# Two-stage mixture of experts: the second stage in 20 slots in place of 23, the last four of them split between two experts

## The reference

```python
logits = jnp.einsum('bsh,eh->bse', x, router_w)
idx = jnp.argmax(logits, axis=-1).reshape(-1)
for e in range(8):
    g = bitlinear(xf, wg[e])                  # rows to int8 steps, weights to -1, 0, 1
    u = bitlinear(xf, wu[e])
    y = bitlinear(jnp.square(jax.nn.relu(g)) * u, wd[e])
    out = out + jnp.where((idx == e)[:, None], y, 0.0)
```

## Time and profile before

| | |
|---|---|
| median of 3 runs | 249.35 us (249.04 to 249.41) |
| profiled execution | 250.49 us |
| its span | 248.4 us |
| busy PE, DVE, ACT, POOL | 90%, 87%, 83%, 67% of the span |
| moved by DMA | 55.94 MB, mean 225 GB/s |

### The profile page before, as it was taken

The page is one execution under the profiler, slowest core; times in us unless marked ns, Lnnn a source line. Parts: engine busy times, 40 slices in busy tenths (PEclk is TensorE's granted clock), DMA queues, the critical chain, the costliest instruction groups (busy, mean ns, idle before and its releaser), DMA issues.

```text
span 248.4 us, 6396 instructions
## 1 busy us (share of the span) xinstructions
PE 224.2 (90%) x1627; PEld 175.1 (70%) x1627; DVE 215.4 (87%) x702; ACT 205.5 (83%) x312; POOL 166.6 (67%) x327
## 2 busy tenths in 40 slices
PE   2398999999999999998999999987799999999970
PEld 2245788889899999998999998974344454544430
DVE  5979999967968999888988999978999999999971
ACT  2768799788767899997999978887779999999970
POOL 4262676746746698888878875555537788687863
PEclk9999999999999999999999999999889999999998
DMA  5999999987955465697566655635068982211110
GB/s 190 424 336 386 428 418 391 369 352 251 367 243 190 154 209 211 225 358 287 198 216 205 221 216 216 211 96 153 24 173 276 298 284 88 106 59 74 64 43 0
DMA packets 14304, 55.94 MB, mean 225 GB/s; under 512 B 2814, under 2 KB 2814, under 8 KB 10176
## 3 DMA queue, kind: packets, MB, share of 16 engines
q1 hardware_dynamic: 9392, 42.10, 47.3%
q0 software_dynamic: 4880, 13.44, 15.5%
HBM read 44.68 MB, written 13.48 MB: 234 GB/s over the span
## 4 chain that ended last, share of the span: by engine, by line
PE 76%; DVE 13%; issue 5%; POOL 2%; ACT 2%; DMA 1%; DVEq 0%; POOLq 0%; ACTq 0%
PE banks L1726 39%; PE banks L1903 20%; PE banks L1709 8%; PE banks L1895 2%; PE banks L2007 2%; PE banks L1871 2%; PE banks L1751 2%; POOL out_rows L719 1%; PE banks L1779 1%; DVE row L1247 1%; DVE ternary L1049 1%; DVE p L1227 1%; DVE stats L1191 1%; DVE hT_lo L1220 1%; DMA token_ids<-token_ids_in 1%
## 5 line engine op out<-in xcount | busy, mean ns | idle before, releaser
L1903 PE MATMUL banks<-ternary,qT 128*128 x184 | 47.6, 389 | 1.5 <-ACT qT L863 1.4
L774 ACT ACTIVATE ternary<-staged 128x2048 bf16<-128x2048 f32 x20 | 38.1, 1905 | 3.1 <-DMA staged<-weight_chunks 3.1
L780 ACT ACTIVATE ternary<-staged,w_scale 128x1536 int16<-128x1536 f32 (+1 forms) x20 | 34.4, 1725 | 2.9 <-DVE w_scale L1144 2.9
L1903 PEld LDWEIGHTS banks<-ternary,qT 128*128 128x128 bf16 x184 | 17.5, 100 | 17.6 <-issue 2.7
L633 POOL DMA_INDIRECT x_rows<-row,store_at x19 | 22.6, 1191 | 9.3 <-POOL store_at L625 6.6
L1726 PE MATMUL banks<-ctx_hi,pT_hi 128*128 x132 | 22.8, 312 | 2.5 <-DVE row L1247 1.1
L1903 PE MATMUL banks<-ternary,rT 128*128 x92 | 23.7, 380 | 1.3 <-ACT rT L887 0.8
L535 POOL DMA_INDIRECT x<-x_rows,gather x16 | 18.3, 1141 | 9.3 <-DVE gather L1061 6.4
L719 POOL DMA_INDIRECT out_rows<-late_rows,late_token x18 | 19.2, 1069 | 7.7 <-DVE late_rows L1498 5.5
L588 POOL TENSOR_TENSOR row<-ln,half_powers 128x2 f32<-128x2 f32 x19 | 14.1, 744 | 13.6 <-DVE squares L1262 13.6
L1726 PE MATMUL banks<-ctx_hi,hT_hi 128*128 x132 | 22.8, 311 | 0.0
(11 more groups left out here) (253 smaller groups left out, 627.2 us busy)
## 6 DMA issues: line engine op xcount, KB each, us to landing
staged<-weight_chunks SPq DMA_DIRECT2D x20, 1024.0 KB, 6.4
late_rows<-x_rows SPq DMA_DIRECT2D x18, 260.0 KB, 3.6
ternary<-ctx_chunks SPq DMA_DIRECT2D x4, 1024.0 KB, 8.2
ternary<-weight_chunks SPq DMA_DIRECT2D x4, 1024.0 KB, 10.0
ternary<-ctx_rows SPq DMA_DIRECT2D x4, 1024.0 KB, 13.0
x_rows<-filler SPq DMA_DIRECT2D x1, 2080.0 KB, 13.9
staged<-x_rows SPq DMA_DIRECT2D x5, 260.0 KB, 3.1
x_rows<-row,store_at POOLq DMA_INDIRECT x19, 3.8
```

Of the source, the lines that this page charges most:

```text
L774: nc.scalar.activation(ternary[:, m * K * D:(m + 1) * K * D], staged_of(i), ACT.Abs, accum_out=abs_sum[:, 2 * i:2 * i + 1]).then_inc(abs_r ...
L780: nc.scalar.activation(ternary[:, m * K * D + first:(m + 1) * K * D].bitcast(I16), staged_of(i)[:, first:], ACT.Copy, scale=w_scale[:, m:m ...
L1903: last = pe.matmul(ps[:, :], side(left[:, :], k), ternary[:, bass.ds(e * (3 * K * D) + (kind * K + k) * D, D)], start=(k == 0), stop=(k == ...
```

## The change

Rows of stage two are counted in halves of 64. There are `B2 = 20` slots: 0 to 15 hold 128 rows of one expert as before (0 to 4 early, 5 to 15 late). Slots 16 to 19 hold two halves of 64 rows which may belong to two experts. In those every product is done as two column tiles: rows 0 to 63 by the expert's matrix in `ternary`, rows 64 to 127 by a copy of the second expert's three matrices (`twin`, 12 KB in each of 128 partitions, one tile for each split slot). SP makes the copies, from on-chip memory to on-chip memory, behind the loads of the two halves of their slot. The tables of the late slots have 18 runs, with a place for each half; their chain has two more pieces, and DVE takes two more of them before `largest_product(1)`. Constants for the halves are made on DVE at tick 10 of stage one. Some tiles of stage one (`x`, `p`, `hT_hi`, `pT_hi`, `pT_lo`, `squares`, `filler` and others) now share memory with tiles of stage two.

```diff
-B2 = TILES + E2 - 1
+HALF = P // 2
+SPLITS = E2 // 2
+SPLIT = TILES
+B2 = SPLIT + SPLITS
-RUNS = 2 * E2 + 1
+RUNS = 2 * (E2 + 1)
-GROUPS = [..., range(11, 15), range(15, 19), range(19, B2)]
+GROUPS = [..., range(11, 15), range(15, 18), range(18, B2)]
+        twin = [sb(f"twin{i}", [P, 3 * K * D], BF16) for i in range(SPLITS)]
...
+            def load_half(s, half):
+                place = s - EARLY + half * SECOND
+                first = sp.value_load(base[1][place:place + 1, 0:1], min_val=0, max_val=SCRATCH_ROWS - HALF)
+                sp.dma_start(cols_of([s], 0, ROW)[half * HALF:(half + 1) * HALF],
+                             x1_rows[bass.ds(first, HALF)]).then_inc(x1_in[s], 16)
+            def copy_matrices(s):
+                place = s - EARLY + SECOND
+                e = sp.value_load(expert2[1][place:place + 1, 0:1], min_val=0, max_val=E2 - 1)
+                sp.dma_start(twin[s - SPLIT][:, :], ternary[:, bass.ds(e * (3 * K * D), 3 * K * D)])\
+                    .then_inc(twin_in[s - SPLIT], 16)
...
-            for s in range(EARLY, B2):
+            for s in range(EARLY, SPLIT):
                 load(s)
+            sp.wait_ge(experts2_ready, 2)
+            sp.wait_ge(cut_ready, MATS)
+            sp.wait_ge(x1_ready, B1)
+            sp.wait_ge(largest_ready, B1)
+            for s in range(SPLIT, B2):
+                for half in range(2):
+                    load_half(s, half)
+                copy_matrices(s)
...
+            def half_constants():
+                at = token1[:, 0:1]
+                first_split = SPLIT - EARLY
+                dve.tensor_scalar(reach_parts[:, 0:1], at, first_split + 0.5, -float(HALF), ALU.is_lt, ALU.mult)
+                dve.tensor_scalar(reach_parts[:, 1:2], at, SECOND + 0.5, float(FAR), ALU.is_gt, ALU.mult)
+                dve.tensor_scalar(reach_parts[:, 2:3], at, SECOND + first_split + 0.5, -float(FAR), ALU.is_gt, ALU.mult)
+                dve.tensor_scalar(half_place[:, :], at, SECOND + 0.5, float(1 - 2 * SECOND), ALU.is_gt, ALU.mult)
+                dve.tensor_scalar(half_row[:, :], at, HALF + 0.5, -float(HALF), ALU.is_gt, ALU.mult)
+                dve.tensor_copy(of_experts(run_expert), iota[:, None, 0:E2].to_broadcast([P, 2, E2]))\
+                    .then_inc(halves_made, 1)
+                dve.wait_ge(halves_made, 1)
+                dve.tensor_reduce(reach[:, :], reach_parts[:, :], X, ALU.add)
+                dve.scalar_tensor_tensor(half_place[:, :], at, 2.0, half_place[:, :], ALU.mult, ALU.add)
+                dve.tensor_tensor(half_row[:, :], half_row[:, :], at, ALU.add).then_inc(halves_made, 1)
+                dve.wait_ge(halves_made, 2)
+                dve.tensor_copy(in_run[1][:, RUNS:], half_place[:, :]).then_inc(halves_made, 1)
...
             def late_slots():
+                next_link(dve.tensor_scalar(pair_end[:, :], half_end[:, :], 0.5, -0.25, ALU.mult, ALU.add))
+                dve.tensor_scalar(run_start[:, singles], half_end[:, :], 1.0, -1.0, ALU.mult, ALU.add)
                 yield
+                after_links()
+                dve.scalar_tensor_tensor(run_halves[:, 0:E2], pair_end[:, :], 2.0, run_start[:, 0:E2],
+                                         ALU.mult, ALU.subtract)
+                next_link(dve.scalar_tensor_tensor(run_halves[:, E2 + 1:], pair_end[:, :], -2.0, half_end[:, :],
+                                                   ALU.mult, ALU.add))
+                yield
+                after_links()
+                next_link(dve.tensor_tensor_scan(late_first[:, 1:], run_halves[:, :], run_floor[:, :], float(PLACE0),
+                                                 ALU.add, ALU.max))
+                yield
+                yield from late_tables()
+                yield from slot_factors(1, RUNS, LATE)
...
-            for _ in range(4):
+            for _ in range(6):
                 next(late)
             largest_product(1)
...
+                    if b < SPLIT:
+                        last = pe.matmul(ps[:, :], rows, ternary[:, columns], start=(k == 0), stop=(k == K - 1))
+                    else:
+                        pe.matmul(ps[0:HALF, :], rows[:, 0:HALF], ternary[:, columns],
+                                  start=(k == 0), stop=(k == K - 1))
+                        last = pe.matmul(ps[HALF:P, :], rows[:, HALF:P],
+                                         twin[b - SPLIT][:, (kind * K + k) * D:(kind * K + k + 1) * D],
+                                         start=(k == 0), stop=(k == K - 1))
...
+                if late:
+                    n = 3 * LATE
+                    pe.matmul(by_slot_ps[1][0:HALF], ones[:, 0:HALF], spread[1][:, 0:n], start=True, stop=True)
+                    last = pe.matmul(by_slot_ps[1][HALF:P], ones[:, HALF:P], spread[1][:, n:], start=True, stop=True)
...
+                if b >= SPLIT:
+                    pe.wait_ge(twin_in[b - SPLIT], 16)
```

More of the change, by code:

```diff
@@ L233, in moe_program @@
             ctx_lo = sb("ctx_lo", [P, E1 * K * WIDTH], F32R)
+            x = [sb(f"x{i}", [P, D], F32) for i in range(RING - 1)]
+            x = [tile[:, :] for tile in x]
+            hT_hi = sb("hT_hi", [P, D], F32R)
+            p = sb("p", [P, D], F32)
+            pT_hi, pT_lo = sb("pT_hi", [P, D], F32R), sb("pT_lo", [P, D], F32R)
+            squares = sb("squares", [P, D], F32)
+            filler = sb("filler", [P, ROW], F32)
+            dump = sb("dump", [P, K * D // SUM_PIECES], BF16)
+            before = sb("before", [P, P], F32)
+            iota16 = sb("iota16", [P, P], F16)
+            abs_sum = sb("abs_sum", [P, 2 * len(ORDER)], F32)
             stack.pop()
@@ L376, in moe_program @@
         x1_in = [sem(f"x1_in{s}") for s in range(B2)]
+        twin_in = [sem(f"twin_in{i}") for i in range(SPLITS)]
+        halves_made = sem("halves_made")
         first_sizes, sizes = sem("first_sizes"), sem("sizes")
@@ L402, in sizes_of, with rows_of @@
             return 3 * min(group, early) + 6 * max(group - early, 0)
+        def rows_of(s):
+            return 16 if s < SPLIT else 32
         def norm2_at(b):
@@ L1342, in slot_factors @@
+            def slot_factors(late, runs, n):
+                one = in_run[late]
                 after_links()
@@ L1423, in mean_products @@
                 yield
-                yield from slot_factors(0, E2, range(EARLY))
+                yield from slot_factors(0, E2, EARLY)
             def quantise(b):
@@ L1612, in _ @@
                     extra_cut(EXTRA_CUT[t])
+                if t == FOLD + 5:
+                    half_constants()
                 if 2 < t != B1 - 1:
@@ L1902, in product2 @@
                         ahead()
-                    last = pe.matmul(ps[:, :], side(left[:, :], k),
-                                     ternary[:, bass.ds(e * (3 * K * D) + (kind * K + k) * D, D)],
-                                     start=(k == 0), stop=(k == K - 1))
+                    rows, columns = side(left[:, :], k), bass.ds(e * (3 * K * D) + (kind * K + k) * D, D)
+                    if b < SPLIT:
+                        last = pe.matmul(ps[:, :], rows, ternary[:, columns], start=(k == 0), stop=(k == K - 1))
+                    else:
+                        pe.matmul(ps[0:HALF, :], rows[:, 0:HALF], ternary[:, columns],
[3 more added lines that the diff above has]
+                                         start=(k == 0), stop=(k == K - 1))
                 return last
```

204 lines of the change are left out of this document (113 added, 91 removed).

## The result

The changed kernel takes 248.71 us (median of 15 runs, 247.46 to 250.17), the kernel before, on the same chips, 249.76 us (15 runs, 249.04 to 250.78). The ratio is 0.9949, 95% interval 0.9932 to 0.9965: faster by 0.5%, 1.3 us by the ratio, where 5.6 us were forecast and the range ended at 247.2. The profiled execution of after has a span of 246.3 us, 2.1 less than before's 248.4.

The account below looks back on a forecast made before the run. TensorE was taken to bound stage two at 2.81 us a slot, DVE and ACT close below. -8.44 + 1.7 + 0.55 + 0.25 + 0.3 = -5.6 us, from 249.35 to 243.7 us; range 241.3 to 247.2.

Parts of the forecast that it names:

- The copies: SP's on-chip copies into `twin`: last lands at 218.7 us, slot 19's gate product needs it at 228.8; cost 0.
- rival 3: Late copies at 9.6 us each: TensorE stands still 8.7 us before slot 19, 252.4 us; chance 6%.
- Three slots fewer, -8.44: Stage two: 23 slots become 20, each worth 2.81 us of TensorE time; -8.44 us.
- Tiles side by side: Split slots 16 to 19: the two column tiles of each product overlap fully, +0 us (bounds +0 and +10.4).
- rivals 1 and 2: Split slots: tiles don't overlap, 254.1 us, chance 6%; or overlap only partly, 246.3 us, chance 8%.
- Switches, 1.7: TensorE going in and out of tiles in slots 16 to 19, 0.21 us a pair of switches; together +1.7 us.
- rival 2: Split slots: partial overlap, a pair of tiles takes a quarter more, 0.27 us, 246.3 us; chance 8%.
- Longer table chain, 0.55 + 0.25: Late tables before `largest_product(1)`: longer DVE chain +0.55 us, one more tiled matmul and pair of switches +0.25 us.
- Ten small instructions in stage one, +0.3: Constants for the halves on DVE at tick 10 delay TensorE's transposes by 0.45 us, partly recovered later; +0.3 us.
- Rival 4, the clock: Near stage two's start: a second lower-clock stretch, +1.7 us (245.4), or the first vanishes (242.0); chance 8%, two thirds loss.

Follow-up runs that it names:

- e1: Changed kernel without the four copies and their waits; second halves multiply by expert 0's matrix in `ternary`; 244.47 us, ratio 0.9796 to the kernel before.
- e8: e1 with whole-array products in place of column tiles in slots 16 to 19, by the first half's expert; 242.52 us, ratio 0.9727.
- e10: Changed kernel with each copy still one transfer but in 1 KB rows, the four twins interleaved in one tile; 249.41 us, ratio 0.9973.
- e2: Kernel before with four copies of 1.5 MB added behind late loads, read by nobody; 254.37 us, ratio 1.0191.
- e5: Changed kernel with `twin` filled by as many bytes from HBM instead of on-chip memory; products read `ternary`; 245.62 us, ratio 0.9820.
- e6: Changed kernel with each copy in three transfers of 4 KB rows instead of one of 12 KB; 246.47 us, ratio 0.9865.
- e7: Changed kernel with each copy in twelve transfers of 1 KB rows; 260.39 us, ratio 1.0441.
- e12: Changed kernel with each copy cut into its three matrices, one issued behind each gate product of slots 7 to 18; 245.26 us, ratio 0.9835.
- e14: e12 with each piece issued behind the slot's up product instead of its gate product; 246.72 us, ratio 0.9884.
- e10b: e10 with rows of 2 KB instead of 1 KB; 248.56 us, ratio 0.9930.

## Why the prediction was wrong

**The step that failed** is "The copies": "Hidden by 10 us, so 0." It asked only when the copies land; that a copy reads the on-chip memory stands in rival 3, but only as a doubt about its rate. The conclusion on landing held, its numbers did not: SP issued the copies at 196.3, 201.5, 208.0 and 214.2 (forecast 197.1 to 208.2), partly because its own register loads between them had grown to about 1 us, and they landed a median 10.1 us later (9.6 us was the bound). The last landed by about 225 where 218.7 was forecast, slot 19's gate product began at 232.57, and nothing waited for `twin`. SP's queue in after, in order of time:

```profile
196.30 0.54 SPq L510 DMA_DIRECT2D twin<-ternary  x1
...
214.18 0.52 SPq L510 DMA_DIRECT2D twin<-ternary  x1
```

The prediction did not ask what else uses the memory that the copies read. Measured, the copies cost 3.9 us in the traces (after's table above), 5.1 - 1.3 = 3.8 us in the times of e1 and after. With 3.9 in place of 0, the sum is -8.44 + 1.7 + 0.55 + 0.25 + 0.3 + 3.9 = -1.7 us, where -1.3 was measured. That it comes so near is in part luck: by after's trace the table chain cost 1.05 in place of 0.8 and stage one ended 0.3 earlier in place of 0.3 later, and with these -8.44 + 1.7 + 1.05 - 0.3 + 3.9 = -2.1, the difference of the two profiled executions. The row that could have warned was in reach but not read: in before the register load stands behind every up product, 0.307 us each, with the range from 303 to 617 ns. The steady 2.81 us a slot hid it, since it was covered. The load of 617 ns starts at 210.00, while POOL's scatter, which reads on-chip memory, is the only traffic and fills the queues (share 0.98, the second to last number); the next, at 212.95, meets none and takes 306 ns. Before in these two moments:

```profile
210.00:210.62 0.62, 0.62 (x6) 0.33 (x5) 0.59 (x2) 0.51 (x2) 0.55 (x1) 1.00 0.98 383
212.95:213.25 0.30, 0.30 (x4) 0.18 (x3) 0.28 (x1) 0.30 (x1) 0.30 (x1) 1.00 0.00 0
```

So before held a price, 0.3 us more for a load. It would have been a bound, not a value: another load, at 201.66, took 0.31 us with the queues full (1.04) and scatter packets among the traffic.

**What held, term by term:**

- *Three slots fewer, -8.44*: from the last split slots to the end, after goes from +6.0 to -2.1 us, and 3 x 2.81 of that is this term; the drain takes 0.3 longer.
- *Tiles side by side* (rivals 1 and 2 are out). TensorE in order of time in slot 17 of after, both halves of a pair:

```profile
225.96 0.41 PE L2016 MATMUL banks<-ternary,qT 128*64 x1
225.96 0.40 PE L2018 MATMUL banks<-twin,qT 128*64 128x512 bf16 x1
226.20 0.38 PE L2016 MATMUL banks<-ternary,qT 128*64 x1
226.20 0.38 PE L2018 MATMUL banks<-twin,qT 128*64 128x512 bf16 x1
```

The two start together, and in the chain of waits the next pair follows after 0.21 us, the step of an undivided product; the first pair of four takes longer:

```profile
227.23 0.33 PE banks L2016
...
227.57 0.21 PE banks L2016
...
228.00 0.21 PE banks L2016
...
228.22 0.22 PE banks L2003 x2
228.43 0.86 PE banks L2014 x4
```

  Four pairs take 0.99 us (227.23 to 228.22) and four whole products 0.86; the transposes behind them take 0.22 in place of 0.11. The sum, 0.13 + 0.11 = 0.24 a pair of switches, is near the 0.21 taken. The drain at a change of mode that the Trainium skill states ("TensorEngine Tiling (Array Packing)", section Tiling Modes) agrees with these numbers. The Trainium skill's figure of 2.38 for three tiles ("TensorE: Matmul & The Clock Gate", section Measured speedup vs the span model), from which rival 2 drew 0.27 us a pair, is for tiles of 32 columns; carried over to two tiles of 64 columns and 512 moving columns it fails: 0.21, and the measurement decides.
- *Switches, 1.7*: three split slots cost 6.02 - 4.66 = 1.36 in the trace (1.26 forecast) and the drain 0.3 more (0.41 forecast, with slot 19's pair); by e8 against e1, 1.7.
- *Longer table chain, 0.55 + 0.25*: DVE's section from `pair_end` (178.55) to the `fac` behind the tables (180.31) takes 1.76 us, 1.19 in before: +0.57. Counted from the end of stage one TensorE is 0.27 + 0.78 = 1.05 us later at the transposes before slot 6, 0.8 forecast. TensorE's wait for it, as forecast by DVE's t, is longer than the 0.74 in the earlier trace rows:

```profile
182.02 0.28 PE L2003 MATMUL banks<-ident,t 128*128 128x128 bf16 x2 [1.67 <-DVE t L1540]
```

- *Ten small instructions in stage one, +0.3*: measured 0. They took 0.95 us of DVE:

```profile
106.03 0.14 DVE L1371 TENSOR_SCALAR reach_parts<-token 128x1 f32<-128x1 f32 x1
...
106.91 0.15 DVE L1383 COPY in_run<-half_place 128x1 f32<-128x1 f32 x1
106.98 0.68 DVE L1215 TENSOR_SCALAR ternary<-ternary 128x2048 bf16<-128x2048 int16 x1
```

  The transposes of `h` began at 109.47 where they began at 109.06, 0.4 later as worked out. But the wait for ACT and DVE that before has at 116.30 to 117.83 is gone: after's products go on at 117.44. The whole 0.4 is given back there and stage one ends 0.3 us earlier; "part of it may vanish there" was the right sentence with the wrong size.
- *Rival 4, the clock*: the granted clock in after's profile is 1.00 at stage two's start, where before had 0.51 for 3.4 us; TensorE waits for DVE's `t` in this place in both (0.74 and 1.67 us), so little was gained. In e10's profile a stretch at the lower clock fell later, where TensorE is the bound. Its stretches before and in it:

```profile
178.60:182.00 3.40, 1.74 (x9) 0.51 (x6) 3.09 (x20) 2.19 (x5) 0.71 (x3) 1.00 0.00 0
183.00:186.40 3.40, 3.30 (x11) 1.25 (x10) 3.19 (x13) 1.98 (x4) 0.38 (x1) 0.57 0.82 217
```

  Twelve products from 183.74 took 4.24 us, where after's twelve took 2.75 (183.55 to 186.30): 1.5 us, near the 1.7 given. TensorE had been busy 1.74 of 3.40 us in the stretch quoted first. After's profile shows 1.62 of 3.40 busy in the same place and no fall, so whether it comes differs between executions or kernels; it may be part of the spread of the runs.

The chances: none of the cases named had this mechanism. Rival 3 was nearest (copies that are not free) but put the cost at a wait for `twin` before slot 19, and priced it at 8.7 us.

**What stays open.** Why a register load is slow while transfers read on-chip memory: what they share in the chip was not taken apart. The load follows transfers out of on-chip memory (e1, e2, e5), their density (e6, e7) and the moment (e12, e14), not packet length (e10, e10b). Density and the number of transfers change together in e6 and e7, so that part is less sharp than the others. A version without copies that keeps the whole computation was not tried.

## What to carry to other kernels

When a change adds transfers, ask not only when they land but which instructions of the bounding engine touch the memory that they read: a register load in the queue of an engine with no slack is one, and it has no busy time in the profile (look for "issue" gaps ahead of the same instruction in each round, then for the source line that stands there). Big copies that nobody is in a hurry for are better cut into pieces and paced by the bounding engine's own progress, so that the load does not fall on the first half microsecond of a piece: e12 got back 2.8 us of 3.9. A steady repeat with no gap says that small costs in it are covered now, not that they are small.

## What the runs showed of the hardware

- A register load of one number from on-chip memory on TensorE takes 0.31 us, and 0.94 to 1.03 us (median; up to 1.48) while transfers from on-chip to on-chip memory fill the DMA queues; with transfers from HBM at the same share (1.00, 377 GB/s) it stays at 0.31 (after, e2, e10 against e5). SP's register load does the same, 0.27 us in e5 and 1.02 in after.
- With copies in pieces of 0.5 MB the register load ends 1.1 to 1.5 us after the piece's first packet (20 loads of e12 and e14): 0.98 us when it starts 0.14 us after it, 0.34 when it starts 0.99 us after it.
- Matmuls and elementwise instructions keep their length while the copies flow (379, 691 and 597 ns from 196 to 222 us in before and after).
- Cutting such a copy into 1 KB rows in one transfer changes the load little, 997 to 944 ns; gaps in time do, 476 ns at a share of 0.82.
- Two column tiles of 64 on bf16 with 512 moving columns run fully side by side, 0.21 us a pair (after); going in and out costs 0.24 us.
